# The opening of a cross attention: where the first rows, the constant rows and the first weights stand in the queues

## The chip, the cores and the metric

The program runs on one core of a Trainium2 chip. The metric is device microseconds for one execution. The kernel before took 2498.39 us (median of 3 runs, 2496.61 to 2503.72). The execution that the profiler recorded took 2492.11 us; its span, from the first to the last instruction, is 2490.3 us.

## The reference

Eight sequences of 512 rows and 512 columns pass through a gated cross attention (16 heads of 32 columns, a bias by relative position, a key mask) and then a gated second block with its own attention and a mixture of experts:

```
x = x + tanh(g_xattn) * Wo(softmax(Q K^T / sqrt(32) + bias[q - k], masked) V)
      with Q = layernorm(x) Wq + bq,  K = ctx Wk + bk,  V = ctx Wv + bv
x = x + tanh(g_ffn) * ffn(layernorm(x))
```

Only the first line matters here, and of it only the work that precedes its first scores.

## The kernel before

The program has three passes, one after the other: pass A is the cross attention, pass B the second attention, pass C the experts. The change is in pass A alone.

Pass A works on one sequence at a time as 64 units (16 heads, in 4 groups of 4, by 4 tiles of 128 keys). Each body of the program has 64 steps. In a step TensorE does one unit's scores, one product for a row minimum of a later unit ("max" in the code, L721), and a piece of a job that prepares the next sequence. Jobs are: XT and CT (transposes of the normalised rows and of the context, four tiles each, L629), Q, K and V (products in four pieces of three matmuls, and one matmul for the bias, L654 and L656), and, later, O, M and SP. The table `plan` gives each job its steps and one of three PSUM banks. TensorE takes jobs in the order of their steps, and one that waits holds up all behind it.

The bodies are called "first" (preparation of sequence 0 only, with max products from step 48), "zero" (units of sequence 0), "steady", "last" and "end". "First" is the opening: it loads rows, splits the four weight matrices into a high and a low half (ScalarE w_hi, L420; VectorE w_lo, L508), makes XT, CT, Q, K, V, and hands Q and K group by group to SyncE. `keep` (L240) stores the two halves of a group to DRAM, waits for that, and `stack` (L248, L253) loads them back three times into `q_stack` and `k_stack`, from which scores and max products read. These stacks also hold constant rows that are loaded once from `side_rows` (L313: one partition; L314: 31 partitions, 496 KB; L315: 22 partitions, 352 KB). Each row of such a source is read 16 times, once for each head.

SyncE issues every load and store of pass A but a few in program order: rows, biases, Wq, Wk, mask, rows again as their two buffers come free, Wv and Wo as the weight buffers come free, mask rows, the constant rows, then `keep` and `stack` by group, the band of the bias (2 MB, L328, after group 0), eight one-row loads (L333, after group 1). The body "zero" begins on SyncE with the loads of the next sequence's rows (L233), which VectorE's statistics need at step 4. GpSimd issues four strip loads of 512 KB and casts them.

Of the kernel before, what the change touches and what calls it, by code (L numbers as in the profile page):

```python
# [19 lines left out]
F32 = mybir.dt.float32  # L20
# [8 lines left out]
P = 128  # L29
# [32 lines left out]
def pass_a(nc, x, ctxt, maskb, g_gate, wq, bq, wk, bk, wv, bv, wo, bo, strips, bands, far, side_rows, ident, x1, mask_rows,  # L62
           qk_rows):

    with ExitStack() as ctx:
# [44 lines left out]
        stats = sb("stats", [P, 2, 6])  # L110
        mv = sb("mv", [P, 2, 2])
        rstd = sb("rstd", [P, 2, 3])
# [7 lines left out]
        mask_stage = o_hi[:, 0, :]  # L120
        far_stage, far_hi, far_lo = den[0:NT * H, :], o_lo[0:NT * H, 0, :], o_lo[0:NT * H, 1, :]
# [11 lines left out]
        c_loaded = [sem(f"c_loaded{i}") for i in range(2)]  # L133
        kept = [sem(f"kept{i}") for i in range(2)]
# [30 lines left out]
        pieces = {j: at for j, at, _ in plan}  # L165
        bank_of = {j: job_bank[i] for j, _, i in plan}
        place = {j: i for j, _, i in plan}
# [5 lines left out]
        done_order = {kind: sorted(js, key=lambda j: (pieces[j][-1], names.index(j))) for kind, js in present.items()}  # L173
# [27 lines left out]
        def ended(kind, step):  # L201
            return [j for j in done_order[kind] if pieces[j][-1] == step]
# [22 lines left out]
        MOMENTS = ((4, 7), (6, 9), (15, 18), (17, 20))  # L225
        SPLITS = (10, 16, 23, 25)
# [4 lines left out]
        def _(sp):  # L231
# [30 lines left out]
            def body(kind, b, u):  # L262
                more, own, late_too = kind in ("first", "zero", "steady"), kind in ("zero", "steady", "last"), kind in ("steady", "last", "end")
                if more:
                    for t in range(2):
                        if kind != "first":
                            sp.wait_ge(job_done, before(kind, b))
# [31 lines left out]
                if more:  # L299
# [5 lines left out]
                if more:  # L305
# [38 lines left out]
        def _(pool):  # L344
            def deviation(b, t):
# [4 lines left out]
                nc.gpsimd.tensor_scalar(rstd[:, t % 2, 0:1], mv[:, t % 2, 1:2], EPS, None, ALU.add).then_inc(rstd_step, 1)  # L350
                pool.wait_ge(rstd_step, done + 1)
                nc.gpsimd.tensor_tensor(rstd[:, t % 2, 1:2], rstd[:, t % 2, 0:1], power[:], ALU.pow).then_inc(rstd_step, 1)
                pool.wait_ge(rstd_step, done + 2)
                pool.nop(nofuse=True)
                nc.gpsimd.tensor_scalar(rstd[:, t % 2, 2:3], mv[:, t % 2, 0:1], rstd[:, t % 2, 1:2], -1.0, ALU.mult, ALU.mult
                                        ).then_inc(rstd_step, 1)

            def body(kind, b, u):
                if kind == "zero":
                    pool.wait_ge(far_stored, 16 * 2 * NT)  # L360
                for step in range(STEPS):
# [13 lines left out]
                    if kind in ("first", "zero", "steady"):  # L375
                        for t, (_, at) in enumerate(MOMENTS):
                            if step == at - 2:
                                deviation(b, t)
                    if kind == "first" and step in (MOMENTS[1][1], MOMENTS[2][1], MOMENTS[3][1], 3 * GS):
                        strips_of((MOMENTS[1][1], MOMENTS[2][1], MOMENTS[3][1], 3 * GS).index(step))  # L380
# [28 lines left out]
            for g in range(2):  # L409
                load_strips(g)  # L410
            pool.wait_ge(const_loaded, 16 * (1 + B))
            nc.gpsimd.tensor_scalar(mask_stage, mask8, MASKED, None, ALU.mult).then_inc(mask_set, 1)
# [4 lines left out]
        def _(act):  # L417
# [5 lines left out]
            def evict(kind, b, u, job):  # L423
# [5 lines left out]
                src = bank_of[job][:]  # L429
# [18 lines left out]
            def body(kind, b, u):  # L448
# [4 lines left out]
                for step in range(STEPS):  # L453
# [11 lines left out]
                    for g in range(NG):  # L465
                        if (M, g) in present[kind] and step == pieces[M, g][0] + 1:
# [3 lines left out]
                    if kind in ("first", "zero", "steady"):  # L470
                        for t, (_, at) in enumerate(MOMENTS):
                            if step == at:
                                act.wait_ge(rstd_step, (b + 1) * (NT * 3) + t * 3 + 3)
                                nc.scalar.activation(xn[:, t % 2, :], xn[:, t % 2, :], ACT.Identity, scale=rstd[:, t % 2, 1:2],
                                                     bias=rstd[:, t % 2, 2:3]).then_inc(xn_ready, 1)
# [22 lines left out]
            act.wait_ge(b_loaded, 128)  # L498
# [6 lines left out]
        def _(dve):  # L505
# [6 lines left out]
            def evict(kind, b, job):  # L512
# [4 lines left out]
                src = bank_of[job][:]  # L517
# [30 lines left out]
            def moments(b, t):  # L548
                dve.wait_ge(x_loaded[t % 2], (b + 1) * 32 + 16 * (t // 2 + 1))
                nc.vector.bn_stats(stats[:, t % 2, :], xn[:, t % 2, :]).then_inc(stats_done, 1)  # L550
                dve.wait_ge(stats_done, (b + 1) * NT + t + 1)
                dve.nop(nofuse=True)
                nc.vector.bn_aggr(mv[:, t % 2, :], stats[:, t % 2, :]).then_inc(mv_done, 1)

            def body(kind, b, u):
                if kind == "zero":
                    dve.wait_ge(band_loaded, 16)
                for step in range(STEPS):
# [23 lines left out]
                    if kind in ("first", "zero", "steady"):  # L582
                        for t, (at, _) in enumerate(MOMENTS):
                            if step == at:
                                moments(b, t)
                    if kind == "first" and step in SPLITS:
                        split(SPLITS.index(step))
                        if step == SPLITS[-1]:
# [4 lines left out]
                    for job in ended(kind, step - 1):  # L593
# [5 lines left out]
            dve.wait_ge(b_split, 2)  # L599
            nc.vector.scalar_tensor_tensor(out=b_lo, in0=bstage[DH:DH + 1], scalar=WS, in1=b_lo, op0=ALU.mult,  # L600
                                           op1=ALU.subtract).then_inc(b_split, 1)
# [3 lines left out]
        def _(pe):  # L605
            mm = nc.tensor.matmul

            def free(kind, b, job):

                mine = [j for j in names if j in present[kind] and place[j] == place[job]]  # L610
                prior = [j for j in mine if pieces[j][0] < pieces[job][0]]
                if prior:
                    last = max(prior, key=lambda j: pieces[j][-1])
                    assert pieces[last][-1] < pieces[job][0], (last, job)
# [6 lines left out]
            def transposes(kind, b, job):  # L621
                m, t = job
                src = cn if m == CT else xn
                if m == CT:
                    pe.wait_ge(c_loaded[t % 2], (b + 1) * 32 + 16 * (t // 2 + 1))
                else:
                    pe.wait_ge(xn_ready, (b + 1) * NT + t + 1)
                for k in range(NK):
                    last = nc.tensor.transpose(bank_of[job][:, k * P:(k + 1) * P], src[:, t % 2, k * P:(k + 1) * P], idn[:])  # L629
                last.then_inc(job_done, 1)  # L630

            def product(kind, b, job, k):

                m, n = job
                o, c = bank_of[job][:], slice(n * P, (n + 1) * P)
# [22 lines left out]
            def spread(kind, b, job):  # L658
# [3 lines left out]
                for hh in range(HG):  # L662
                    last = mm(bank_of[job][hh * DH:(hh + 1) * DH, :], ones_f[:], acc[:, hh, :], start=True, stop=True,
# [3 lines left out]
            def turn_low(kind, b, job):  # L667
# [3 lines left out]
                for i in range(NT):  # L671
                    last = nc.tensor.transpose(bank_of[job][0:HG, i * P:(i + 1) * P], low[:, g % 2, i * HG:(i + 1) * HG], idn[:])
                last.then_inc(job_done, 1)

            def fill(kind, b, step):

                for job in names:
                    if job not in present[kind]:
                        continue
                    for k, at in enumerate(pieces[job]):  # L680
# [1774 lines left out]
```

## Time and profile before

| | |
|---|---|
| median of 3 runs | 2498.39 us |
| profiled execution | 2492.11 us, span 2490.3 us |
| TensorE busy | 2193.2 us, 88% of the span |
| TensorE busy in the first 120 us | 59.92 us |
| TensorE busy from 120 to 200 us | 73.89 of 80 us |
| first max product | at 76.31 us |
| first max product of body "zero" | at 93.61 us |

A row of the timeline gives start, duration, engine, line, operation, output and inputs, and in brackets the idle time before it with what ended it. SPq is SyncE issuing a DMA; the duration is that of the issue, not that of the transfer. A row of the windows gives busy time and count for each engine, then the granted clock (1.00 is 2.4 GHz, 0.50 is 1.2 GHz), the mean busy share of the 16 DMA engines (one engine alone is 0.06), and the rate.

### The profile page before, as it was taken

What the parts mean: (1) busy time and instruction counts of PE and PEld (TensorE: products, weight loads), DVE (VectorE), ACT (ScalarE), POOL (GpSimd) and SP (SyncE); (2) the same over time, 40 slices, a digit from 0 to 9 for tenths busy, and PEclk for the clock granted to TensorE, in tenths of its full rate; (3) what the DMA queues carried; (4) which work ended last, traced back from release to release, by engine and by line L of the source; (5) the groups of instructions that cost most, each with busy time, mean ns of one, the idle gap of its engine ahead of it and who ended that gap; (6) DMA issues with size and microseconds to landing.
All of it is one profiled execution on the core that took longest, in us unless ns stands there. A gap on an engine that the chain in (4) does not pass through costs nothing. (4 is left out here: it accounts for less than half of the span.)

```text
span 2490.3 us, 50414 instructions
## 1 busy us (share of the span) xinstructions
PE 2193.2 (88%) x12864; PEld 977.9 (39%) x12865; DVE 1506.9 (61%) x4072; ACT 1201.2 (48%) x2316; POOL 1401.2 (56%) x1598
## 2 busy tenths in 40 slices
PE   3699999999999963899999999999948887898887
PEld 1233333333333211444444444444424443444443
DVE  4588888887888733656655566565526783333332
ACT  3255555555555433354544545455445653444443
POOL 3177767677676751365654655546534664555554
PEclk9899999999999986999999999999978898999999
DMA  4413223232232204452533524334234764555554
GB/s 155 151 48 111 90 87 109 72 107 96 86 116 71 71 26 130 140 147 86 151 118 111 147 90 146 116 118 130 80 107 86 165 148 91 97 93 93 94 92 79
DMA packets 221402, 264.60 MB, mean 106 GB/s; under 512 B 37400, under 2 KB 163468, under 8 KB 220852
## 3 DMA queue, kind: packets, MB, share of 16 engines
q1 hardware_dynamic: 197628, 212.81, 28.2%
q0 software_dynamic: 22976, 48.38, 11.3%
q8 instruction: 106, 1.74, 0.3%
q14 instruction: 172, 1.41, 0.2%
q10 hardware_dynamic: 520, 0.27, 0.0%
HBM read 162.12 MB, written 86.80 MB: 100 GB/s over the span
## 5 line engine op out<-in xcount | busy, mean ns | idle before, releaser
L464 ACT ACTIVATE a_pt<-a_bank 128x512 f32<-128x512 f32 x512 | 305.1, 597 | 361.2 <-DVE a_bank L567 349.2
L1345 DVE CUSTOM_DVE_ANT_0 b_bank<-b_bank,b_tri 128x256 f32<-128x256 f32 (+3 forms) x512 | 253.7, 498 | 322.2 <-PE b_bank L1483 319.8
L578 DVE CUSTOM_DVE_ANT_0 a_bank<-a_bank,a_strip 128x512 f32<-128x512 f32 x512 | 354.8, 693 | 21.5 <-PE a_bank L721 18.8
L1130 POOL TENSOR_TENSOR b_acc<-b_acc,b_pt 128x256 f32<-128x256 f32 (+2 forms) x384 | 271.7, 725 | 105.6 <-ACT b_pt L1219 88.9
L374 POOL TENSOR_TENSOR a_acc<-a_acc,a_pt 128x512 f32<-128x512 f32 x256 | 317.6, 1271 | 12.8 <-ACT a_pt L464 9.3
L567 DVE TENSOR_TENSOR a_bank<-a_bank,a_band 128x256 f32<-128x256 f32 (+1 forms) x512 | 205.9, 403 | 132.3 <-PE a_bank L708 130.5
L1219 ACT ACTIVATE b_pt<-b_bank 128x256 f32<-128x256 f32 (+2 forms) x384 | 143.3, 381 | 203.5 <-PE b_bank L1467 199.5
L721 PE MATMUL a_bank<-a_k_stack,a_q_stack 97*128 97x512 f16 x512 | 197.7, 387 | 17.5 <-DMA a_k_stack<-mask_rows 10.7
L708 PE MATMUL a_bank<-a_q_stack,a_k_stack 128*128 128x512 f16 x512 | 197.6, 387 | 15.4 <-ACT a_pt L464 11.4
L1812 POOL DMA_INDIRECT out_dram<-c_z,c_to_row x72 | 115.1, 1598 | 144.1 <-DMA out_dram<-c_z,c_to_row 117.0
L2203 DVE SCALAR_TENSOR_TENSOR c_hid<-c_th,c_bank 128x256 f32<-128x256 f32 x72 | 30.3, 421 | 229.6 <-ACT c_th L1954 228.2
L1465 PE MATMUL b_bank<-b_q_stack,b_k_stack 96*128 96x256 f16 (+3 forms) x512 | 155.5, 304 | 8.7 <-ACT b_pt L1219 7.8
L371 POOL TENSOR_TENSOR a_acc<-a_pt 128x512 f32<-128x512 f32 x128 | 160.0, 1271 | 5.3 <-ACT a_pt L464 4.9
L1482 PE MATMUL b_bank<-b_k_stack,b_q_stack 96*128 96x256 f16 (+3 forms) x512 | 154.5, 302 | 5.0 <-DMA b_q_stack<-qk_rows 2.7
L388 POOL TENSOR_TENSOR a_o_un<-a_o_un,a_den 128x512 f32<-128x512 f32 x32 | 40.8, 1275 | 204.1 <-DVE a_den L534 204.1
L1145 POOL TENSOR_TENSOR b_o_un<-b_o_un,b_den 128x512 f32<-128x512 f32 x32 | 40.7, 1273 | 201.6 <-DVE b_den L1313 195.6
L1467 PE MATMUL b_bank<-b_q_stack,b_k_stack 97*128 97x256 f16 (+3 forms) x512 | 153.3, 300 | 0.0
L1483 PE MATMUL b_bank<-b_k_stack,b_q_stack 96*128 96x256 f16 (+3 forms) x512 | 153.0, 299 | 0.0
L1927 ACT ACTIVATE c_z<-c_z,c_entry 128x512 f32<-128x512 f32 x72 | 51.9, 721 | 192.9 <-DMA c_z<-z_all,c_from_row 192.9
L735 PE MATMUL a_bank<-a_pt,a_v 128*32 128x512 f32 x1024 | 138.5, 613 | 1.1 <-ACT a_pt L464 1.1
L708 PEld LDWEIGHTS a_bank<-a_q_stack,a_k_stack 128*128 128x128 f16 x512 | 49.5, 97 | 186.3 <-ACT a_pt L464 117.5
L1219 ACT ACTIVATE b_acc<-b_bank 128x512 f32<-128x512 f32 x128 | 76.4, 597 | 94.4 <-PE b_bank L1467 94.3
(337 smaller groups left out, 5632.7 us busy)
## 6 DMA issues: line engine op xcount, KB each, us to landing
b_q_stack<-qk_rows SPq DMA_DIRECT2D x192, 128.0 KB, 2.7
a_q_stack<-qk_rows SPq DMA_DIRECT2D x96, 128.0 KB
a_k_stack<-qk_rows SPq DMA_DIRECT2D x96, 128.0 KB
b_k_stack<-qk_rows SPq DMA_DIRECT2D x96, 128.0 KB, 2.6
a_xn<-in_x SPq DMA_DIRECT2D x32, 256.0 KB, 2.6
a_cn<-in_ctx SPq DMA_DIRECT2D x32, 256.0 KB, 3.1
qk_rows<-a_qk_hi SPq DMA_DIRECT2D x64, 128.0 KB, 1.7
qk_rows<-a_qk_lo SPq DMA_DIRECT2D x64, 128.0 KB, 1.8
```

What stands on the lines that cost most here:

```text
L371: nc.gpsimd.tensor_tensor(acc[:, hh, :], pt[:, (n - HG) % SLOTS, :], mine, ALU.add).then_inc(pooled, 1)
L374: nc.gpsimd.tensor_tensor(acc[:, hh, :], acc[:, hh, :], mine, ALU.add).then_inc(pooled, 1)
L464: nc.scalar.activation(pt[:, n % SLOTS, :], st_bank[n % 2][:], ACT.Exp).then_inc(exped, 1)
L567: nc.vector.tensor_tensor(st_bank[n % 2][:, c0:c1], st_bank[n % 2][:, c0:c1], band[:, h, at:at + c1 - c0], ALU.add).then_inc(biased, 1)
L578: nc.vector.tensor_tensor_reduce(out=max_bank[step % 2][:], in0=max_bank[step % 2][:], in1=strip[:, g * HG + hh, at:at + S], scale=-1.0, s ...
L708: mm(st_bank[n % 2][:], k_stack[:, h, j * P:(j + 1) * P], q_stack[:, h, :], start=True, stop=True).then_inc(scored, 1)
L721: mm(max_bank[step % 2][:], q_stack[0:MASK + 1, h, i * P:(i + 1) * P], k_stack[0:MASK + 1, h, :], start=True, stop=True).then_inc(maxed, 1)
L1130: nc.gpsimd.tensor_tensor(sums_of, sums_of, probs(n), ALU.add).then_inc(pooled, 1)
L1219: nc.scalar.activation(probs(n), st_bank[n % 2][:, 0:w], ACT.Exp).then_inc(exped, 1)
L1345: nc.vector.tensor_tensor_reduce(out=max_bank[step % 2][:, 0:w], in0=max_bank[step % 2][:, 0:w], in1=tri[:, at:at + w], scale=-1.0, scalar ...
L1465: mm(o, k_stack[0][0:LOW, h, j * P:(j + 1) * P], q_stack[0][0:LOW, h, j * P:], start=True, stop=False)
L1482: mm(o, q_stack[0][0:LOW, h, c], k_stack[0][0:LOW, h, 0:w], start=True, stop=False)
```

## The change

Only the body "first" is different in what it issues; the other bodies keep their plan.

- All eight row tiles of sequence 0 are loaded at once: the third and fourth of x go to `sums`, those of the context to the upper halves of `o_hi` and `o_lo`. Order on SyncE: four x tiles, Wq, four context tiles, Wk, gate, mask, far rows, the constant rows, Wv, and then `keep` of Q group 0.
- The biases are loaded by four DMAs from ScalarE's queue instead of eight from SyncE's.
- Statistics of the four x tiles come at steps 0 to 3, and VectorE does them before the low half of the biases. GpSimd issues its first strip loads after them and does all strips in one go.
- A plan of its own: XT at steps 4 to 7, Q group 0 at 8, CT at 12 to 15, then K, V, Q, K, V, Q, K at steps up to 47, V group 2 at 50 to 56, on six banks.
- `stack` of Q group 0 comes before the mask rows and Wo are issued, and the wait for the mask rows stands before `stack` of K.

```
+        first_plan = [((XT, 0), [4], 0), ((XT, 1), [5], 1), ((XT, 2), [6], 2), ((XT, 3), [7], 3), ((Q, 0), run(8), 4),
...
+        places = job_bank + st_bank + [out_bank]
...
-        SPLITS = (10, 16, 23, 25)
+        FIRST_MOMENTS = ((0, 0, 1), (1, 1, 2), (2, 2, 3), (3, 3, 4))
+        SPLITS, LOW_SPLITS = (3, 16, 22, 34), (4, 18, 24, 36)
...
                 if kind == "first":
-                    for n, w in enumerate((bq, bk, bv, bo)):
-                        for row in (0, DH):
-                            sp.dma_start(bstage[row:row + 1, n, :], w.rearrange("(a n) -> a n", a=1)).then_inc(b_loaded, 16)
+                    for t in range(NT):
+                        sp.dma_start(x_tile(kind, t), x[0, t * P:(t + 1) * P, :]).then_inc(x_first[t - 2] if t >= 2 else x_loaded[t], 16)
                     weights(0)
+                    for t in range(NT):
+                        sp.dma_start(c_tile(kind, t), ctxt[0, t * P:(t + 1) * P, :]).then_inc(c_first[t - 2] if t >= 2 else c_loaded[t], 16)
                     weights(1)
...
                 if kind == "first":
-                    weights(2)
-                    weights(3)
-                    sp.wait_ge(mask_set, 1)
-                    sp.dma_start(mask_rows, mask_stage).then_inc(mask_stored, 16)
                     sp.dma_start(q_stack[MASK:MASK + 1, :, :], side_rows[0:1]...).then_inc(sides_stored, 16)
                     sp.dma_start(k_stack[LOW:, :, :], side_rows[1:]...).then_inc(sides_stored, 16)
                     sp.dma_start(q_stack[SIDE + 2 * NT:, :, :], side_rows[SIDE + 2 * NT - MASK:]...).then_inc(sides_stored, 16)
-                    sp.wait_ge(mask_stored, 16)
+                    weights(2)
...
                         keep(kind, b, b + 1, g, part)
+                        if kind == "first" and g == 0:
+                            for i in range(2):
+                                sp.sem_inc((x_loaded, c_loaded)[part][i], 16)
+                            if part:
+                                sp.wait_ge(mask_stored, 16)
                         stack(b + 1, g, part)
+                        if kind == "first" and g == 0 and part == 0:
+                            sp.wait_ge(mask_set, 1)
+                            sp.dma_start(mask_rows, mask_stage).then_inc(mask_stored, 16)
+                            weights(3)
```

The order on SyncE, from the context tiles on, before the change (a_pt is the buffer in which weights land, qk_rows the DRAM copy of Q and K):

```order
L233 DMA a_xn<-in_x 128x512 [waits a_job_done] x2
L233 DMA a_cn<-in_ctx 128x512 [waits a_job_done] x2
L259 DMA a_pt<-in_L_xattn_Wv 128x4x512 [waits a_w_split]
L259 DMA a_pt<-in_L_xattn_Wo 128x4x512 [waits a_w_split]
L312 DMA mask_rows<-a_o_hi 128x512 [waits a_mask_set]
L313 DMA a_q_stack<-in_side_rows 1x16x512
L314 DMA a_k_stack<-in_side_rows 31x16x512
L315 DMA a_q_stack<-in_side_rows 22x16x512
L240 DMA qk_rows<-a_qk_hi 128x512 [waits a_left_dve,a_mask_stored]
```

And the same place after it, from the load of Wk:

```order
L287 DMA a_pt<-in_L_xattn_Wk 128x4x512
L304 DMA a_gate<-in_g_xattn 128x1
L306 DMA a_o_un<-in_mask_BxS_bf 16x128 x8
L307 DMA a_den<-in_beyond 64x512
L337 DMA a_q_stack<-in_side_rows 1x16x512
L338 DMA a_k_stack<-in_side_rows 31x16x512
L339 DMA a_q_stack<-in_side_rows 22x16x512
L287 DMA a_pt<-in_L_xattn_Wv 128x4x512 [waits a_w_split]
L268 DMA qk_rows<-a_qk_hi 128x512 [waits a_left_dve]
L276 DMA a_q_stack<-qk_rows 32x4x512 [waits a_kept0]
L358 DMA mask_rows<-a_o_hi 128x512 [waits a_mask_set]
L287 DMA a_pt<-in_L_xattn_Wo 128x4x512 [waits a_w_split]
```

Wv stood ahead of the 31 constant rows and stands behind them; Wo and the mask rows moved behind the first stack of Q.

On TensorE, where the max products begin, before the change (the products with a_w_hi first are those of V):

```order
L656 MATMUL a_bank<-a_ones,a_bias 128x512
L721 MATMUL a_bank<-a_k_stack,a_q_stack 128x512
L654 MATMUL a_bank<-a_w_hi,a_ct_hi 128x512
L654 MATMUL a_bank<-a_w_lo,a_ct_hi 128x512
L654 MATMUL a_bank<-a_w_hi,a_ct_lo 128x512
L721 MATMUL a_bank<-a_k_stack,a_q_stack 128x512
```

And after it:

```order
L695 MATMUL a_bank<-a_ones,a_bias 128x512
L760 MATMUL a_bank<-a_k_stack,a_q_stack 128x512 x3
L693 MATMUL a_bank<-a_w_hi,a_ct_hi 128x512
L693 MATMUL a_bank<-a_w_lo,a_ct_hi 128x512
L693 MATMUL a_bank<-a_w_hi,a_ct_lo 128x512
L760 MATMUL a_bank<-a_k_stack,a_q_stack 128x512 x2
```

Before, V group 1, Q group 2, K group 2 and V group 2 ran among the 16 max products; now only V group 2 does, and the other three stand ahead of them.

## Rows read from the trace of the kernel before

**Rows 1.** Windows of three stretches of pass A: engines, clock, DMA share, GB/s.
```profile
0.00:120.00 120.00, 59.92 (x244) 26.93 (x245) 54.89 (x105) 34.12 (x45) 30.10 (x44) 0.91 0.48 152
...
120.00:200.00 80.00, 73.89 (x396) 27.64 (x397) 66.43 (x183) 45.00 (x80) 57.49 (x52) 0.98 0.21 65
200.00:1100.00 900.00, 816.84 (x4393) 317.30 (x4392) 672.94 (x1810) 450.76 (x809) 572.85 (x551) 0.95 0.30 95
```

**Rows 2.** Waits of TensorE in the first 120 us, longest in total first.
```profile
PE a_bank L629 <- ACT a_xn L474: 22.6, 1, 22.6
PE a_bank L629 <- DVE a_xt_lo L545: 14.4, 4, 6.5
PE a_bank L721 <- DMA a_k_stack<-mask_rows: 10.7, 1, 10.7
PE a_bank L721 <- DVE a_low L578: 6.8, 2, 6.0
```

**Rows 3.** Timeline of SyncE's queue, 36 to 76 us.
```profile
37.50 0.44 SPq L314 DMA_DIRECT2D a_k_stack<-in_side_rows  x1
37.99 21.41 SPq L315 DMA_DIRECT2D a_q_stack<-in_side_rows  x1
59.51 1.14 SPq L240 DMA_DIRECT2D qk_rows<-a_qk_hi  x1
...
68.90 1.29 SPq L248 DMA_DIRECT2D a_q_stack<-qk_rows  x3
...
73.06 1.29 SPq L248 DMA_DIRECT2D a_k_stack<-qk_rows  x3
...
74.72 0.35 SPq L328 DMA_DIRECT2D a_band<-in_bands  x1
```

**Rows 4.** Windows of the DMA load, same columns as rows 1.
```profile
0.00:16.00 16.00, 0.00 (x0) 0.01 (x1) 2.90 (x4) 5.10 (x3) 1.63 (x8) 1.00 0.85 278
...
40.00:42.00 2.00, 1.66 (x8) 1.56 (x8) 0.28 (x1) 0.51 (x1) 1.70 (x3) 1.00 0.60 220
...
46.00:48.00 2.00, 0.00 (x0) 0.00 (x0) 2.00 (x1) 1.14 (x3) 0.00 (x0) 1.00 0.06 20
...
66.00:68.00 2.00, 0.00 (x0) 0.00 (x0) 0.00 (x0) 0.26 (x1) 0.00 (x0) 1.00 0.07 24
```

**Rows 5.** Timeline of the split of Wk, on ScalarE and VectorE.
```profile
31.65 1.90 ACT L420 ACTIVATE a_w_hi<-a_pt 128x2048 f16<-128x2048 f32 x1
...
33.59 2.29 DVE L508 SCALAR_TENSOR_TENSOR a_w_lo<-a_pt,a_w_hi 128x2048 f16<-128x2048 f32 x1 [1.11 <-ACT a_w_hi L420]
```

**Rows 6.** Timeline of TensorE and VectorE around the first max products.
```profile
76.31 0.61 PE L721 MATMUL a_bank<-a_k_stack,a_q_stack 97*128 97x512 f16 x1 [10.68 <-DMA a_k_stack<-mask_rows]
...
82.56 0.38 PE L654 MATMUL a_bank<-a_w_hi,a_ct_lo 128*128 128x512 f16 x1
82.77 0.38 PE L656 MATMUL a_bank<-a_bias,a_ones 128*128 128x512 f16 x1
...
93.61 0.60 PE L721 MATMUL a_bank<-a_k_stack,a_q_stack 97*128 97x512 f16 x2
...
84.39 0.70 DVE L578 CUSTOM_DVE_ANT_0 a_bank<-a_bank,a_strip 128x512 f32<-128x512 f32 x1
...
86.12 0.70 DVE L578 CUSTOM_DVE_ANT_0 a_bank<-a_bank,a_strip 128x512 f32<-128x512 f32 x1
```

**Rows 7.** Windows of the two stretches at a lowered clock.
```profile
76.00:82.00 6.00, 5.69 (x14) 2.09 (x15) 2.82 (x7) 0.00 (x0) 0.00 (x0) 0.50 0.86 317
...
106.00:113.00 7.00, 4.20 (x10) 1.30 (x11) 5.78 (x17) 3.35 (x6) 2.11 (x6) 0.52 0.38 132
```

**Rows 8.** Timeline of SyncE, VectorE and TensorE at the next sequence's rows.
```profile
104.00 0.35 SPq L233 DMA_DIRECT2D a_xn<-in_x  x1
...
100.52 0.14 DVE L578 DVE_READ_ACCUMULATOR2_ANT a_low<- 128x1 f32 x1
107.01 0.69 DVE L550 BATCH_NORM_STATS2 a_stats<-a_xn 128x6 f32<-128x512 f32 x1 [6.35 <-DMA a_xn<-in_x]
```

More of the change, by code:

```diff
@@ L133, in pass_a @@
         c_loaded = [sem(f"c_loaded{i}") for i in range(2)]
+        x_first = [sem(f"x_first{i}") for i in range(2)]
+        c_first = [sem(f"c_first{i}") for i in range(2)]
         kept = [sem(f"kept{i}") for i in range(2)]
@@ L164, in pass_a, with pieces, place, bank_of @@
                 ((K, 2), run(56), 0), ((V, 2), [60, 60, 61, 61], 1)]
-        pieces = {j: at for j, at, _ in plan}
-        bank_of = {j: job_bank[i] for j, _, i in plan}
-        place = {j: i for j, _, i in plan}
+        first_plan = [((XT, 0), [4], 0), ((XT, 1), [5], 1), ((XT, 2), [6], 2), ((XT, 3), [7], 3), ((Q, 0), run(8), 4),
+                      ((CT, 0), [12], 5), ((CT, 1), [13], 0), ((CT, 2), [14], 1), ((CT, 3), [15], 2), ((K, 0), run(18), 3),
+                      ((V, 0), run(24), 1), ((Q, 1), run(28), 0), ((K, 1), run(32), 2), ((V, 1), run(36), 1), ((Q, 2), run(40), 0),
+                      ((K, 2), run(44), 2), ((V, 2), [50, 52, 54, 56], 1)]
+        places = job_bank + st_bank + [out_bank]
+        plans = {kind: {j: (at, i) for j, at, i in (first_plan if kind == "first" else plan)}
+                 for kind in ("first", "zero", "steady", "last", "end")}
+        def pieces(kind, j):
+            return plans[kind][j][0]
+        def place(kind, j):
+            return plans[kind][j][1]
+        def bank_of(kind, j):
+            return places[place(kind, j)]
         names = [j for j, _, _ in plan]
@@ L201, in ended @@
         def ended(kind, step):
[L202 removed]
+            return [j for j in done_order[kind] if pieces(kind, j)[-1] == step]
         def adds(n):
@@ L224, in pass_a, with moments_at, x_tile, c_tile @@
         STEPS = UNITS
-        MOMENTS = ((4, 7), (6, 9), (15, 18), (17, 20))
-        SPLITS = (10, 16, 23, 25)
+        MOMENTS = ((4, 5, 7), (6, 7, 9), (15, 16, 18), (17, 18, 20))
+        FIRST_MOMENTS = ((0, 0, 1), (1, 1, 2), (2, 2, 3), (3, 3, 4))
+        SPLITS, LOW_SPLITS = (3, 16, 22, 34), (4, 18, 24, 36)
+        def moments_at(kind):
+            return {"first": FIRST_MOMENTS, "zero": MOMENTS, "steady": MOMENTS, "last": (), "end": ()}[kind]
+        def x_tile(kind, t):
+            return x_spare[t - 2] if kind == "first" and t >= 2 else xn[:, t % 2, :]
+        def c_tile(kind, t):
+            return c_spare[t - 2] if kind == "first" and t >= 2 else cn[:, t % 2, :]
         block = ctx.enter_context(nc.Block())
@@ L298, in body @@
                         stack(b, G3, part)
-                if more:
+                if kind in ("zero", "steady"):
                     for m, t in ((XT, 0), (XT, 1), (CT, 0)):
@@ L304, in body @@
                     store(0)
-                if more:
+                if kind in ("zero", "steady"):
                     sp.wait_ge(job_done, upto(kind, b, (CT, 1)))
@@ L374, in body @@
                             nc.gpsimd.tensor_tensor(acc[:, hh, :], acc[:, hh, :], mine, ALU.add).then_inc(pooled, 1)
[L375 to L380, printed above, removed]
+                    for t, (_, at, _) in enumerate(moments_at(kind)):
+                        if step == at:
+                            deviation(b, t)
+                    if kind == "first" and step == FIRST_MOMENTS[-1][1]:
+                        for g in range(2):
+                            load_strips(g)
+                        pool.wait_ge(const_loaded, 16 * (1 + B))
+                        nc.gpsimd.tensor_scalar(mask_stage, mask8, MASKED, None, ALU.mult).then_inc(mask_set, 1)
+                        for g in range(NG):
+                            strips_of(g)
                     g, off = divmod(step, GS)
@@ L469, in body @@
                                           ).then_inc(m_stacked[g], 16)
[L470 to L475, printed above, removed]
+                    for t, (_, _, at) in enumerate(moments_at(kind)):
+                        if step == at:
+                            act.wait_ge(rstd_step, (b + 1) * (NT * 3) + t * 3 + 3)
+                            nc.scalar.activation(x_tile(kind, t), x_tile(kind, t), ACT.Identity, scale=rstd[:, t, 1:2],
+                                                 bias=rstd[:, t, 2:3]).then_inc(xn_ready, 1)
                     if kind == "first" and step in SPLITS:
@@ L581, in body @@
                                                        accum_out=low[:, g % 2, i * HG + hh:i * HG + hh + 1]).then_inc(lowered, 1)
[L582 to L588, printed above, removed]
+                    for t, (at, _, _) in enumerate(moments_at(kind)):
+                        if step == at:
+                            moments(kind, b, t)
+                    if kind == "first" and step == FIRST_MOMENTS[-1][0]:
+                        dve.wait_ge(b_split, 2)
+                        nc.vector.scalar_tensor_tensor(out=b_lo, in0=bstage[DH:DH + 1], scalar=WS, in1=b_lo, op0=ALU.mult,
+                                                       op1=ALU.subtract).then_inc(b_split, 1)
+                    if kind == "first" and step in LOW_SPLITS:
+                        split(LOW_SPLITS.index(step))
+                        if step == LOW_SPLITS[-1]:
                             dve.wait_ge(gate_ready, 1)
```

77 lines of the change are left out of this document (39 added, 38 removed).

## The prediction

> **What bounds the kernel now.** I read the windows first: the first 120 us keep TensorE busy for 59.92 us, the next 80 for 73.89, and the 900 after that for 816.84 [rows 1]. Past the opening TensorE is the bound, and its work there is not touched, so whatever the opening saves moves everything behind it earlier. Next the waits of TensorE in those 120 us: 22.6 us until the first normalised tile, 14.4 for single evictions between transposes, 10.7 before the first max product, 6.8 near the start of body "zero" [rows 2]. The last two are the ones that stand directly before work that nothing can overtake, so the question is what releases them.
>
> Then SyncE's timeline. It issues the 31 constant rows at 37.50 and then needs 21.41 us to issue the 22 rows. So `keep` of Q group 0 is issued at 59.51, and its `stack` only at 68.90; K follows at 73.06 and the band at 74.72 [rows 3]. The windows of the DMA load tell what it waited for: from 46 to 60 us, in seven windows of 2 us, and again from 64 to 68, the 16 engines are busy to 0.06 to 0.07, one sixteenth, at 20 to 24 GB/s [rows 4]. One engine alone carries the 31 rows. Its backlog begins when the bulk loads end, at about 41 (the window 40 to 42 falls to 0.60), and ends just before 68.3, as the stack starts at 68.90: 27.3 us. SyncE is released at 59.4, 18.4 us after that beginning. I call this one engine's backlog the lane.
>
> The Trainium skill ("DMA: Bandwidth & Descriptors", "Why a DMA increments its semaphore by 16 and not by 1") says that a transfer spreads over the largest number of engines, at most 16, that divides its slowest dimension, and over the lowest-numbered ones. By that rule 31 partitions give one engine and 22 give eleven; the trace agrees with its 0.07 of 16.
>
> **The change part by part.**
>
> *Rows, statistics, biases, own plan.* TensorE's 22.6 us wait for the first tile and the 14.4 us between transposes shrink or go. I cost this at nothing, gained or lost, for the lane covers it. Even if Wk were split no earlier than before, at 33.59 + 2.29 = 35.9 [rows 5], and Q and K group 0 ran only then, 26 matmuls at the slow pace of 0.446 us that rows 6 show (below), they would be done at 47.5, when Wv lands. Without that cover this part would be worth up to the 16 us by which Q and K can be ready before 47.
>
> *Constant rows ahead of Wv and of `keep`.* They wait for nothing now, so the lane begins when the bulk ahead of it has passed. The first 16 us moved 278 GB/s x 16 us = 4.4 MB before [rows 4]; now x, ctx, Wq and Wk are 4 MB, with 0.3 MB of small loads and part of 1 MB of strips. I take 16 us again, as the start of the lane. It lasts 27.3 us, plus one more strip load's sixteenth, 32 KB at 24 GB/s = 1.3 us (two fall into it now, one did before). Wv's sixteenth is 64 KB, 2.7 us, and `keep`, 16 KB or 0.7 us of the 27.3, is now behind it. That a transfer behind the lane waits for it is in the rows: `keep`, issued at 59.51, has landed only at 68.90, while the other engines have nothing from 64 on [rows 3, 4]. Wv has landed at 16 + 27.3 + 1.3 + 2.7 - 0.7 = 46.6, say 47 us. SyncE itself is stuck until 16 + 18.4 + 1.3 = 36; it could not issue Wv before, and Wv's other fifteen parts are in by about 42. The gain is that the lane ends near 45 instead of 68; the price is that Wv, which landed before the lane, now lands after it.
>
> *From Wv to the first max product.* After it ScalarE w_hi 1.90 and VectorE w_lo 2.29 follow one another [rows 5]: 47 + 4.3 with the hand-overs = 51.3. Then V, Q, K, V, Q, K stand in TensorE's order before step 48: 6 x 13 = 78 matmuls. From 82.56 to 93.61 there are 51 starts, 0.217 us each [rows 6]: 16.9 us. TensorE has idled before, as it had before 76.31, where the granted clock was 0.50, its 1.2 GHz level [rows 7], and 14 starts took 6.25 us instead of 3.0 [rows 6]: 3.2 more. The first max product comes at 51.3 + 16.9 + 3.2 = 71.4, before at 76.31: **4.9 us gained**. `stack` of K does not hold it: Q is kept at about 47.7, stacked at 49, mask rows and Wo are issued at 50, `keep` of K at 51; 1.8 MB at the 278 GB/s of the first stretch is 6.5 us, so `stack` of K is issued at 57.5 and lands near 60. The same queue held the wait for mask rows before; those are stored by then.
>
> *The 16 max steps.* Before, 52 matmuls of four jobs ran among them, from 76.31 to 93.61: 17.3 us. Now 13. VectorE sets the pace: two steps from 84.39 to 86.12, 0.865 us each [rows 6], 16 of them 13.8 us. **3.5 us gained**, and body "zero" begins at 85.2 instead of 93.61.
>
> *The next sequence's rows.* Before, SyncE reached them at 104.00, and VectorE stood 6.35 us from 100.66 to 107.01 [rows 8]. From the band at 74.72 to 107.01 is 32.3 us, and nearly all of it is SyncE's own chain (band, two groups, eight one-row loads), which the change leaves as it is. It starts at about 58 now, and the rows are in at 90.3. VectorE needs them 7.0 us after the first max product of "zero", at 92.2. **6.35 us gained**, with 1.9 us to spare; if the chain is later than that, it takes back what it is late.
>
> *The clock after that stall.* The stretch 106 to 113 had 10 matmuls at 0.52 [rows 7], 2.0 us slower than at full rate; VectorE was busy for 5.78 of the 7 us, so I count half, **1.0 us gained**.
>
> *Rest.* ScalarE's four bias DMAs, the later strips (needed at 71) and the split of Wo (issued at 50, due at about 60) lie beside the lane or the six jobs. Semaphore increments, other banks: nothing measurable, bounded by 0 and the 0.7 us of one hand-over each side. None of them stands last before TensorE.
>
> Sum: 4.9 + 3.5 + 6.35 + 1.0 = 15.7 us. Against the profiled execution 2492.11 - 15.7 = 2476.4; the median of before lies 6.3 us above that execution, so I give 2498.39 - 15.7 = **2482.7 us**.
>
> Unknown costs, both ends. The lane: 496 KB at 24 GB/s would be 20.7 us instead of 27.3, which gives 6.6 us more; with all four strips in it and half the surplus again it is 34 us, which takes 6.7 us away, from the first max product and (less the 1.9) from the stall. I keep 27.3, the measured length. Start of the lane: 14 to 18 us. The slow clock before V group 0: 0 to 3.2 us, I take 3.2.
>
> The same page ("Queues, rings and completion order") says that each engine takes its ring's entries in order. By it Wv's sixteenth sits behind the 31 rows, and the trace agrees, as `keep` does [rows 3, 4]; without it Wv would be in at 42, and the sum 18 us, since the next sequence's rows would then be late by 2.8. It speaks against a change that puts Wv there.
>
> **The rivals.**
>
> One: the lane is short, or Wv does not share it. For it: 496 KB at the rate seen make 20.7 us only. Then Wv lands at 42, the max products begin at 66.4, and SyncE's chain ends at 86 to 90. The gain is 18 to 22 us: about 2478. Against it: the measured 27.3.
>
> Two: the lane is longer, because four strip loads and the end of the bulk loads fall into it. Every us goes through at full price at the first max product, and after 1.9 us also at the next rows, but there it replaces, not adds. With a lane end 8 us later the gain is 15.7 - 8 = 8: 2490.7. For it: the first 16 us moved at 0.85 of the engines, so something always shares engine 0.
>
> Three: no change. The early Q and K are of no use, SyncE holds Wv until far later than 36, and Wv lands at 60. TensorE would begin the max products at 84, but the stall and the 3.5 us are still won: 15.7 - 13 = 2.7 us gained, 2495.7.
>
> Four, on the other side: Wv behind the lane makes it slower. It is the place of Wv in the queue: 47 us now, while it stood ahead of the lane before. The point from which this decides is Wv landing at 47 + 15.7 = 63; it is slower by 0.3% from 70. For that the lane must run at half the measured rate, 12 GB/s, 55 us: Wv at 74, gain 15.7 - 27 = -11: 2510. For it: the transfer's 27.3 us against 20.7 by bytes show that sharing costs. Against it: seven windows at a constant 24 GB/s.
>
> **How the numbers follow.** My forecast (gain 12 to 18 us) has 0.50, rival one 0.19, rival two 0.18, rival three 0.08, rival four 0.05. A measurement of this kernel can tell about 0.3%, 7.5 us. Faster by more than that: 0.50 + 0.19 + 0.16 of two = 0.85; within it: the rest of two, three and a part of four, 0.12; slower 0.03. The range: rival one's end and the lane's lower bound give 2473; two gives 2491, and some of three is taken in up to 2493.
>
> **What would show it.** Right: the issue of the 22 rows again lasts about 20 us, from 12.7 on; a stretch of 0.07 DMA share between 20 and 45; TensorE idle until about 51, then six jobs in a row, the first of them at a clock of 0.5; first max product at 71, "zero" at 85; no wait of the statistics for rows in "zero". Wrong: a first max product released by a DMA of `k_stack` instead of by K group 2 (then SyncE's chain decides, not Wv); a stall of the statistics of more than 3 us; Wv in before 42 or after 55; or a stretch after 200 us that takes longer than before.

## The result, and the profile after

The changed kernel takes 2486.34 us (median of 6 runs, 2480.95 to 2491.43), the kernel before, run beside it, 2498.19 us (6 runs, 2493.34 to 2503.72). The ratio is 0.995 with an interval of 0.9932 to 0.9969: it is faster by 11.9 us, less than the 15.7 forecast and inside the range. The profiled execution took 2480.95 us with a span of 2479.2, 11.1 us less than before.

The windows answer to [rows 1].

```profile
0.00:120.00 120.00, 70.40 (x296) 29.63 (x297) 62.49 (x137) 40.55 (x58) 40.67 (x57) 0.87 0.51 161
120.00:200.00 80.00, 77.60 (x418) 28.20 (x417) 66.63 (x184) 45.30 (x81) 56.41 (x51) 1.00 0.24 77
200.00:1100.00 900.00, 816.75 (x4431) 319.44 (x4430) 669.76 (x1805) 454.18 (x818) 571.35 (x546) 0.96 0.31 96
```

TensorE's busy time from 200 to 1100 us is the same as before, 816.75 against 816.84. The whole difference lies in the first 200 us, where more work is done earlier. SyncE's timeline, and then windows of the DMA load, against [rows 3, 4]:

```profile
14.04 0.50 SPq L338 DMA_DIRECT2D a_k_stack<-in_side_rows  x1
14.58 24.13 SPq L339 DMA_DIRECT2D a_q_stack<-in_side_rows  x1
38.75 1.30 SPq L287 DMA_DIRECT2D a_pt<-in_L_xattn_Wv  x1
...
52.38 1.29 SPq L276 DMA_DIRECT2D a_q_stack<-qk_rows  x3
...
92.17 0.35 SPq L261 DMA_DIRECT2D a_xn<-in_x  x1
```

```profile
18.00:20.00 2.00, 1.05 (x3) 0.44 (x4) 0.89 (x2) 0.00 (x0) 0.56 (x1) 1.00 0.70 230
20.00:22.00 2.00, 2.00 (x6) 0.69 (x5) 0.00 (x0) 0.00 (x0) 2.00 (x3) 1.00 0.11 41
22.00:24.00 2.00, 2.00 (x10) 0.97 (x9) 0.00 (x0) 0.06 (x1) 2.00 (x2) 1.00 0.07 24
...
34.00:36.00 2.00, 2.00 (x6) 0.76 (x5) 0.00 (x0) 0.00 (x0) 1.32 (x2) 0.50 0.07 24
...
48.00:50.00 2.00, 0.00 (x0) 0.00 (x0) 0.00 (x0) 0.00 (x0) 0.00 (x0) 0.50 0.07 26
```

The backlog of the one engine now begins right behind the bulk loads, at about 19.5 (the window 18 to 20 still has 0.70), and still holds at 48 to 50, with Wv's sixteenth at its end. Wv was issued at 38.75 and is not in before 51.6. The Trainium skill's rule that each engine takes its ring's entries in order ("DMA: Bandwidth & Descriptors", "Queues, rings and completion order") agrees with this.

The timeline of ScalarE, VectorE and TensorE from the eviction of K group 0 to the first exponential:

```profile
36.81 0.60 ACT L471 ACTIVATE a_qk_hi<-a_bank 128x512 f16<-128x512 f32 x1 [8.53 <-PE a_bank L695]
51.66 1.91 ACT L453 ACTIVATE a_w_hi<-a_pt 128x2048 f16<-128x2048 f32 x1 [14.25 <-DMA a_pt<-in_L_xattn_Wv]
...
53.60 2.29 DVE L542 SCALAR_TENSOR_TENSOR a_w_lo<-a_pt,a_w_hi 128x2048 f16<-128x2048 f32 x1 [15.47 <-ACT a_w_hi L453]
...
55.99 0.58 PE L693 MATMUL a_bank<-a_w_hi,a_ct_hi 128*128 128x512 f16 x1 [19.22 <-issue]
...
75.05 0.60 PE L760 MATMUL a_bank<-a_k_stack,a_q_stack 97*128 97x512 f16 x2
...
87.03 0.38 PE L760 MATMUL a_bank<-a_k_stack,a_q_stack 97*128 97x512 f16 x1 [0.39 <-DVE a_low L615]
...
95.35 0.69 DVE L587 BATCH_NORM_STATS2 a_stats<-a_xn 128x6 f32<-128x512 f32 x1 [1.02 <-DMA a_xn<-in_x]
...
97.34 0.60 ACT L497 ACTIVATE a_pt<-a_bank 128x512 f32<-128x512 f32 x1 [8.04 <-DVE a_bank L604]
```

ScalarE waited 14.25 us for Wv and nothing else. TensorE had Q and K of group 0 done and then stood for 19.22 us. The view puts this down to "issue", but its first matmul starts 0.1 us after w_lo ends (53.60 + 2.29). The first max product follows 78 matmuls later with no wait for a stack, where before it waited 10.7 us for one [rows 2].

One correction to what stands ahead. The row at 93.61 [rows 6] holds the last two max products of "first", not the first of "zero". There are 16 of them from 76.31, two of them in that row, and the first one of "zero" is this, in the timeline of the kernel before:

```profile
95.04 0.38 PE L721 MATMUL a_bank<-a_k_stack,a_q_stack 97*128 97x512 f16 x1 [0.83 <-DVE a_low L578]
...
109.00 0.60 ACT L464 ACTIVATE a_pt<-a_bank 128x512 f32<-128x512 f32 x1 [12.01 <-DVE a_bank L567]
```

So the 16 steps took 18.7 us before, not 17.3. With it the gain adds up as follows (all times in us, read off the two profiled executions):

| stretch | before | after | gained | forecast |
|---|---|---|---|---|
| start to first max product | 76.31 | 75.05 | 1.3 | 4.9 |
| 16 max steps | 18.7 | 12.0 | 6.7 | 3.5 |
| "zero" to the statistics of the next rows | 12.0 | 8.3 | 3.7 | 6.35 |
| to the first exponential | 2.0 | 2.0 | 0.0 | |
| from there to the end of the span | | | -0.6 | 1.0 |
| sum | | | 11.1 | 15.7 |

### The profile page after: what moved, and what is told of

Its sections match the earlier page's. It is cut to its first block and busy times, and to the rows that moved or that the text cites. A ratio compares the mean times of both kernels' runs of the same rounds, so it can differ in the third digit from the quotient of the medians.

```text
span 2479.2 us, 50415 instructions
## 1 busy us (share of the span) xinstructions
PE 2192.0 (88%) x12864; PEld 976.4 (39%) x12865; DVE 1503.3 (61%) x4072; ACT 1200.4 (48%) x2316; POOL 1401.9 (57%) x1598
## 5 line engine op out<-in xcount | busy, mean ns | idle before, releaser
L407 POOL TENSOR_TENSOR a_acc<-a_acc,a_pt 128x512 f32<-128x512 f32 x256 | 317.8, 1271 | 10.7 <-ACT a_pt L497 7.5
```

The lines of the kernel that those rows point to most:

```text
L407: nc.gpsimd.tensor_tensor(acc[:, hh, :], acc[:, hh, :], mine, ALU.add).then_inc(pooled, 1)
```

## The experiments

The theory: the backlog of one DMA engine (the lane) decides when Wv is in, and with it everything up to the first max product. Its rivals: the gain comes from the early x and Q whatever the lane does; SyncE's own chain (`keep`, `stack`, band, next rows) decides; or the lane's length, not its place, is all that counts. Ratios are against the kernel before on the same chip: for the first four kernels its median is 2496.78 us (22 runs), for the others 2497.07 (11 runs). Beside the changed kernel it was 2498.19, so a plain difference from the changed kernel's median comes out 1.1 to 1.4 us larger than one taken through the kernel before.

### The lane spread over all engines

```
-  sp.dma_start(k_stack[LOW:, :, :], side_rows[1:]...broadcast_to([P - LOW, H, S]))
+  sp.dma_start(k_stack[LOW:LOW + 16, :, :], side_rows[1:17]...broadcast_to([16, H, S]))
+  sp.dma_start(k_stack[LOW + 16:, :, :], side_rows[17:]...broadcast_to([P - LOW - 16, H, S]))
```

The 31 rows become 16 and 15, with TensorE waiting for one more increment. In the changed kernel:

> The changed kernel with the 31 constant rows loaded by two DMAs, 16 rows and 15 rows, instead of one. Theory (one engine's backlog decides): the stretch with a DMA share of 0.07 disappears, SyncE issues the 22 rows in under 1 us, Wv has landed by 26 instead of 51.66, the first max product comes at about 60 instead of 75.05, the statistics of the next sequence at about 79 instead of 95.35, and the time falls by 14 to 18 us against the changed kernel. Rival (what held Wv was the bulk of bytes before it, not one engine): Wv lands 5 us earlier at most and the time falls by under 5 us.

Measured: 2471.42 us (6 runs, 2468.29 to 2476.53), ratio 0.99 (0.9883 to 0.9918), so 14.9 us below the changed kernel (13.5 if each is taken against the kernel before that ran beside it). The 22-row issue takes 0.31 us, and Wv is no longer what ScalarE waits for (SyncE's queue, then ScalarE and VectorE):

```profile
14.42 0.31 SPq L340 DMA_DIRECT2D a_q_stack<-in_side_rows  x1
16.80 0.40 SPq L287 DMA_DIRECT2D a_pt<-in_L_xattn_Wv  x1
...
36.97 0.60 ACT L472 ACTIVATE a_qk_hi<-a_bank 128x512 f16<-128x512 f32 x1 [8.32 <-PE a_bank L696]
37.46 1.90 ACT L454 ACTIVATE a_w_hi<-a_pt 128x2048 f16<-128x2048 f32 x1
...
81.02 0.69 DVE L588 BATCH_NORM_STATS2 a_stats<-a_xn 128x6 f32<-128x512 f32 x1 [0.32 <-DMA a_xn<-in_x]
...
83.01 0.60 ACT L498 ACTIVATE a_pt<-a_bank 128x512 f32<-128x512 f32 x1 [7.65 <-DVE a_bank L605]
```

w_hi comes 14.2 us earlier than after the change (37.46 against 51.66), now right behind the eviction of K group 0, and the first exponential 14.3 us earlier. This shows the lane as the bound of the changed opening. The trace agrees with the Trainium skill's rule on the number of engines ("DMA: Bandwidth & Descriptors", "Why a DMA increments its semaphore by 16 and not by 1"), which the prediction cited: sixteen partitions go over sixteen engines, and of the long stretch of 0.07 one window of 0.08 is left, at 34 to 36.

The same edit in the kernel before:

> The kernel before with the same split of the 31 rows. Theory: Q group 0 is kept at 57 instead of 68.9, the first max product comes at about 66 instead of 76.31, SyncE's chain then ends with the next sequence's rows at about 95 instead of 107.01, and the time falls by about 12 us (9 to 14), as much as the whole change gave. Rival (the gain of the change came from its early x and Q): the split alone gives under 4 us.

Measured: 2487.13 us (10 runs, 2482.85 to 2495.42), ratio 0.9964 (0.9949 to 0.9978), 9.7 us gained. The first max product is at 66.47, released by the mask rows of the stack after 1.16 us, and the statistics of the next rows still wait (VectorE):

```profile
96.71 0.70 DVE L551 BATCH_NORM_STATS2 a_stats<-a_xn 128x6 f32<-128x512 f32 x1 [8.88 <-DMA a_xn<-in_x]
```

The four kernels make a square: without the split the change is worth 11.9 us, with it 2487.13 - 2471.42 = 15.7. The split is worth 9.7 before and 13.5 after, each against its own kernel before. The profiled executions say the same by the time of the first exponential (109.00 before, 98.70 with the split, 97.34 changed, 83.01 changed with the split): the change is worth 11.7 and 15.7, the split 10.3 and 14.3. The 3.8 us between 11.9 and 15.7 are less than the intervals of these medians can tell, so that the lane covers part of the change's worth rests on one execution of each kernel.

The rival's own mark, under 4 us for the split alone, is missed. But the square does not take the early x and Q out of the account: with the lane spread in both kernels, the other parts of the change still gain 15.7. No run has the early rows with the constant rows left at their old place, so how the 11.9 us divide between the rows, the plan and the place of the lane is not shown.

### Place of the lane: Wv ahead of it

```
 if kind == "first":
+    weights(2)
     sp.dma_start(q_stack[MASK:MASK + 1, :, :], ...)
     ...
-    weights(2)
```

> The changed kernel with Wv issued ahead of the constant rows, nothing else. Theory that SyncE's chain stands just behind Wv: V group 0 follows K group 0 at once and the first max product comes at about 65.5 instead of 75.05, but stack of K group 0 stays at 62 and the next sequence's rows still arrive at 95 to 97, so the time stays within 2 us of the changed kernel's. Rival (Wv alone decides, as the prediction's sum has it): the time falls by about 9 us.

Measured: 2487.32 us (7 runs, 2481.89 to 2491.58), ratio 0.996 (0.9945 to 0.9976), which overlaps the changed kernel's 0.9932 to 0.9969: no change that can be told. The first max product comes at 68.47, 6.6 us earlier than in the changed kernel, but the stall comes back:

```profile
93.24 0.69 DVE L587 BATCH_NORM_STATS2 a_stats<-a_xn 128x6 f32<-128x512 f32 x1 [5.68 <-DMA a_xn<-in_x]
```

5.68 us of waiting instead of 1.02: what Wv gives, SyncE's chain takes. With Wv out of the lane the statistics begin only 2.1 us earlier (93.24 against 95.35), and the first exponential, too, at 95.22 instead of 97.34. So the lane holds the changed kernel at two places, and freeing one of them brings out the other.

### The lane early in the kernel before

```
     sp.dma_start(far_stage, far).then_inc(far_loaded, 16)
+    (the three loads of constant rows)
     ...
     sp.dma_start(mask_rows, mask_stage).then_inc(mask_stored, 16)
-    (the three loads of constant rows)
```

> The kernel before with only one part of the change: the three DMAs of constant rows stand behind the far rows and ahead of the second half of the rows, Wv and Wo. Theory: the one-engine backlog runs from 16 to 44, but SyncE is stuck in it until about 38, so the third row tile arrives about 17 us later than before, Q group 0 is evicted near 70, and the time rises by about 3 us (0 to 7): the early place pays only with all rows loaded ahead. Rival (the early place is by itself the gain): the time falls by 10 us or more.

Measured: 2502.38 us (10 runs, 2498.16 to 2505.47), ratio 1.0019 (1.0007 to 1.0032), 5.6 us slower. SyncE's queue says why:

```profile
13.29 20.37 SPq L282 DMA_DIRECT2D a_q_stack<-in_side_rows  x1
33.70 2.43 SPq L233 DMA_DIRECT2D a_xn<-in_x  x1
```

The third x tile is behind the stuck issue, VectorE waits 16.38 us for it, and the first exponential comes at 112.42 instead of 109.00. Moving the constant rows forward alone is a loss; in the change all eight row loads stand ahead of them.

### Both behind the lane moved: Wv first and the next rows early

```
-  if kind in ("zero", "steady"):
+  if kind == "steady":
       (loads of the next rows)
   ...
   if kind == "first" and g == 1:
+      sp.wait_ge(job_done, upto("first", -1, (CT, NT - 1)))
+      for t in range(2):
+          load(x, xn, x_loaded, 0, t)
+          load(ctxt, cn, c_loaded, 0, t)
```

This stands on top of the kernel with Wv first.

> The changed kernel with Wv ahead of the constant rows, and with the first four row loads of the next sequence issued after the stacks of group 1 and before the one-row loads, instead of at the end of SyncE's chain. Theory (with Wv first, SyncE's chain is the next limit): the 5.68 us stall of the statistics goes, the first exponential comes at about 89.5 instead of 95.22, and the time falls by 4 to 6 us against the kernel with Wv first alone. Rival (those rows were late for another reason, such as the queue's bytes): under 1.5 us.

Measured: 2479.72 us (5 runs, 2476.19 to 2479.98), ratio 0.9925 (0.991 to 0.994): 7.6 below the kernel with Wv first, more than the 4 to 6 expected. The statistics have no wait at all, at 91.75. But in this execution the issue of the 22 rows lasted 25.25 us, and Wo came late on ScalarE's timeline:

```profile
61.92 1.91 ACT L457 ACTIVATE a_w_hi<-a_pt 128x2048 f16<-128x2048 f32 x1 [12.65 <-DMA a_pt<-in_L_xattn_Wo]
...
64.35 0.57 ACT L475 ACTIVATE a_qk_hi<-a_bank 128x512 f16<-128x512 f32 x1
```

The evictions of Q, V and K stand behind this split in ScalarE's order, and TensorE waited 10.4 us for them. So the first max product is at 72.61 and the first exponential at 93.73 instead of the 89.5 expected. That the rows were the second bound is shown by the wait that is gone. In this execution Wo's split is the third. The size is not explained: the first exponential is only 1.5 us earlier than with Wv first (95.22), and the two profiled executions differ by 2.2 us (2481.89, the lowest of its seven, and 2479.72), where the medians differ by 7.6. The lane differs from execution to execution (below).

### The strips' share of the lane

```
-  for g in range(2):
-      load_strips(g)
   pool.wait_ge(const_loaded, 16 * (1 + B))
   nc.gpsimd.tensor_scalar(mask_stage, mask8, MASKED, None, ALU.mult)...
+  pool.wait_ge(mask_stored, 16)
+  for g in range(2):
+      load_strips(g)
```

In the changed kernel GpSimd issued 1 MB of strips at 13.59, just ahead of the lane. Here they wait until the mask rows are stored.

> The changed kernel with the four strip loads of 512 KB issued only after the mask rows are stored, so that none runs before or beside the 31 constant rows. Theory (the term that was too small in the prediction is the strips' share on the one engine, 128 KB at 24.5 GB/s): Wv lands 5 us earlier, at about 46.5, the first max product comes at about 70 instead of 75.05; the strips then collide with Wo, so the chain gains less, and the first exponential comes 2 to 4 us earlier. Rival (the backlog is as long without them): Wv lands within 1 us of 51.66.

Measured: 2480.38 us (6 runs, 2477.32 to 2485.84), ratio 0.9931 (0.9915 to 0.9946), 6.0 below the changed kernel. That interval overlaps the changed kernel's 0.9932 to 0.9969, so a gain in time is not shown. What the run can show is in its timeline, with Wv's split and the statistics:

```profile
46.44 1.91 ACT L454 ACTIVATE a_w_hi<-a_pt 128x2048 f16<-128x2048 f32 x1 [7.37 <-DMA a_pt<-in_L_xattn_Wv]
...
93.51 0.69 DVE L588 BATCH_NORM_STATS2 a_stats<-a_xn 128x6 f32<-128x512 f32 x1 [5.12 <-DMA a_xn<-in_x]
```

Wv is in 5.2 us earlier, and the first max product is at 69.31, 5.7 us earlier. The first exponential moves by 1.85 us only, because the statistics wait 5.12 us again. The profiled execution, 2485.84 us, is the slowest of the six and no faster than the changed kernel's median.

### The way to a faster kernel

On top of the spread lane: the next rows early, as above, and V group 1, Q group 2 and K group 2 put back between the max products.

```
-  ((V, 1), run(36), 1), ((Q, 2), run(40), 0), ((K, 2), run(44), 2), ((V, 2), [50, 52, 54, 56], 1)]
+  ((V, 1), run(48), 1), ((Q, 2), run(52), 0), ((K, 2), run(56), 2), ((V, 2), [60, 60, 61, 61], 1)]
```

> The changed kernel with the 31 rows split in two DMAs, the early row loads, and V group 1, Q group 2 and K group 2 back among the 16 max products as before the change. Theory (six jobs ahead of the max products cost more than they save, since VectorE's 0.75 to 0.87 us a step leaves room for three matmuls): the max products begin at about 53 instead of 61.42, the first of body zero at 69 instead of 73.4, the first exponential at about 78.5 instead of 83.01, and the time falls by 3 to 6 us against the split alone. Rival (the jobs slow the max steps by as much as they come earlier): within 1.5 us.

Measured: 2464.71 us (4 runs, 2460.89 to 2467.06), ratio 0.9864 (0.9846 to 0.9882), 6.7 below the spread lane alone (whose interval begins at 0.9883) and 21.6 below the changed kernel. The early rows and the other order of the jobs were not tried one without the other here. The first max product is at 52.51, as expected, but the 16 steps took 19.8 us, since VectorE had other work ahead of them:

```profile
52.33 2.29 DVE L547 SCALAR_TENSOR_TENSOR a_w_lo<-a_pt,a_w_hi 128x2048 f16<-128x2048 f32 x1 [1.11 <-ACT a_w_hi L458]
54.54 0.15 DVE L635 TENSOR_SCALAR a_gate<-a_gate 128x1 f32<-128x1 f32 x1
54.60 0.67 DVE L637 TENSOR_TENSOR a_o_lo<-a_den,a_o_lo 64x512 f16<-64x512 f32 x1
```

TensorE waited 2.2 us for VectorE, and the granted clock of 56 to 60 was 0.58. So the first exponential, 79.73, is 3.3 us earlier than with the spread lane, where 4.5 were expected.

Last, Wv ahead of the constant rows in this kernel:

> All of these together: the split, Wv ahead of the constant rows, early row loads, jobs among the max products. Theory: V group 0 follows K group 0 at 37 without a wait, the max products begin when K group 0 is stacked, at about 50, the first exponential comes at about 75, and the time is 6 to 9 us under the split alone, near 2463. Rival (K group 0's stack and the 31 rows share the same bytes, so Wv first only moves the wait): no more than split, rows and jobs give without Wv first.

Measured: 2465.57 us (4 runs, 2462.85 to 2469.88), ratio 0.9869 (0.9852 to 0.9886): no difference, as the rival forecast. The theory's times did not come: the first max product is at 53.59 instead of 50 and the first exponential at 80.75 instead of 75, both 1.0 to 1.1 us later than without the move. The rival's reason, shared bytes, was not tested. In the rows ScalarE splits Wv right behind the eviction of K group 0 in both kernels, so an earlier Wv has no taker. Once the lane is spread, Wv's place in the queue costs nothing that can be told.

## Why the prediction was right, and where it was not

**The bound: right.** The first max product was released by the jobs behind Wv, and Wv by the lane. Spreading the lane alone took 13.5 to 14.9 us away, and no other single edit of the changed kernel took as much. The issue of 22 rows lasted about 20 us as forecast (24.13), the 0.07 windows are there, TensorE idled and began at the slow clock. The price named in the prediction, that Wv now lands after the lane and not before it, is real: with Wv ahead of the lane the first max product comes at 68.47, 6.6 us earlier.

**The lane's start: the term that was mis-sized.** The prediction took 16 us for the start, the value of the kernel before. The windows show the bulk ending at about 19.5, 3.5 us later. In the kernel before, the first two strip loads were issued at 1.35 and lay within the first 16 us. Now they are issued at 13.59, just ahead of the lane, and 4.3 + 1 MB at the prediction's 278 GB/s make an estimated 19 us. The third and fourth (24.65 and 28.98) fall into the lane, as the prediction had it: one is in its 27.3 us, one it added as 1.3. The sum with the true start gives 46.6 + 3.5 = 50.1, and Wv's split began at 51.66; the last 1.5 us are less than the lane differs from one execution to the next. All four strips together are 128 KB on the lane's engine, an estimated 5.2 us at the 24 to 26 GB/s of the windows. Held back, they gave that back: 46.44. The first term was 1.3 instead of 4.9. That is rival two at half its size.

**From Wv to the first max product: right.** Forecast 16.9 + 3.2 = 20.1 us for 78 matmuls, measured 75.05 - 55.99 = 19.1. The 3.2 us for the slow clock came from a miscount: from 76.31 to 82.56 there are 15 starts in the timeline before, not 14, so the slow pace is 0.417 us and not 0.446. Here the slow start cost 19.1 - 16.9 = 2.2 us.

**The 16 max steps: right in kind, wrong in size, twice.** They began at a mis-read end (18.7 us before, not 17.3), 1.4 us to the good. And the pace of 0.865 us was not VectorE's, as the prediction put it. It is TensorE's: one max product and three matmuls of a job at 0.217 us each make 0.87, and in 14 of the 16 steps before there stood job matmuls. VectorE alone does a step in 0.65 to 0.70, as these three of the changed kernel show, and in the changed kernel 12 of the 16 steps have no job; the mean is 12.0 / 16 = 0.75.

```profile
84.08 0.70 DVE L615 CUSTOM_DVE_ANT_0 a_bank<-a_bank,a_strip 128x512 f32<-128x512 f32 x1
...
84.77 0.70 DVE L615 CUSTOM_DVE_ANT_0 a_bank<-a_bank,a_strip 128x512 f32<-128x512 f32 x1
...
85.43 0.70 DVE L615 CUSTOM_DVE_ANT_0 a_bank<-a_bank,a_strip 128x512 f32<-128x512 f32 x1
```

The four slow steps at 1.2 GHz before [rows 7] are gone too, as the forecast had it, since the clock rises in V group 0 now. The gain was 6.7 instead of 3.5.

**The stall of the next rows: gone but for 1.02 us.** Forecast were rows at 90.3 and need at 92.2. SyncE issued them at 92.17 and the statistics began at 95.35. SyncE's chain is late by the lane, not by Wv: the band was issued at 63.74 where 58 was forecast, and with Wv first the chain stayed nearly where it was and the wait is 5.68. The need is later than forecast as well. The 7.0 us behind the first max product of "zero" were counted from the mis-read 93.61; from 95.04 they are 5.6. In the changed kernel they are 7.3, from 87.03 to 94.33. What the stretch gained, 3.7 us, is less than the 5.3 that the stall lost, and the rest is a stretch at a lowered clock which the prediction did not have, the windows of 88 to 92 in the changed kernel:

```profile
88.00:92.00 4.00, 4.00 (x14) 1.59 (x13) 1.32 (x5) 0.59 (x1) 0.00 (x0) 0.60 0.54 167
```

Before, this part of "zero" (95 to 107) ran at a granted clock of 0.97. Ahead of the fall TensorE had gone through the steps without jobs, waiting for VectorE at nearly every one. This is the row of its waits in the first 120 us; one of the 12, 0.64 us at 97.11, lies behind the fall, so that 11 waits with 3.5 us in total stand ahead of it:

```profile
PE a_bank L760 <- DVE a_low L615: 4.2, 12, 0.7
```

The other kernels sort the same way. In the 4 us that begin about 1 us after the first max product of "zero", the granted clock was 0.57 with the spread lane, 0.66 with Wv first, 0.57 with the next rows early as well and 0.70 with the strips held back, all with the same steps without jobs. It was 1.00 in that place in the kernel before, in its two variants, and in the last two kernels, all of which have jobs among the steps. That the waiting itself brings the clock down was not tried alone. The term of 1.0 us for the clock after the stall did not show: behind the first exponential nothing more was gained, and 0.6 us were lost up to the end of the span.

**Order of the rivals.** Rival one (short lane) and rival four (slower) are excluded by the windows and the time. Rival three is excluded by Wv, which is in at 51.6 and not at 60; how much the early Q and K are worth by themselves stays open, as said at the square. The forecast was 3.8 us too high in gain: 3.6 and 2.7 and 1.6 too much in the three terms above (first max, stall, clock and rest), and 3.2 too little in the max steps, which leaves 4.6 for the profiled span. That the total came so close is in part luck: of 7.9 us too much, 3.2 were made up by a misread row and a pace taken too slow.

## What to carry to other kernels

A load over 31 partitions made one engine a queue of its own here. Look for windows of 0.06 to 0.07 and for an issue of 20 us on the next DMA, and cut the load into 16 and the rest before moving anything around it. An early place in a queue is worth only what stands behind it. Row loads behind the lane cost 5.6 us, and Wv behind it held the first max product back by 6.6 us; putting Wv back gained no time until the next rows were moved as well. When a stretch gets shorter, count who waits in it: in all five kernels here where TensorE waited a little at nearly every step, it ran at a lower clock right after.

## What the runs showed of the hardware that was not expected

The spread lane moves its bytes on all engines, but slowly. The windows of the changed kernel with the split:

```profile
22.00:24.00 2.00, 2.00 (x7) 0.76 (x6) 0.00 (x0) 0.00 (x0) 2.00 (x2) 1.00 1.06 116
24.00:26.00 2.00, 2.00 (x18) 1.70 (x16) 1.07 (x2) 1.70 (x4) 1.70 (x4) 1.00 1.18 103
26.00:28.00 2.00, 0.01 (x1) 0.00 (x0) 2.00 (x4) 2.00 (x3) 2.00 (x2) 1.00 1.03 99
```

The mean share is at 1 (it can come out above 1 in this view), at 99 to 116 GB/s. In the next window, 28 to 30, with what was queued behind, Wv among it, it is 299 at a share of 1.04. One engine alone moved 24 to 26. So the rate in these windows, which hold a strip load as well, is about four times that of one engine, not sixteen times. Whether it is the few destination partitions, or the source row of 1 KB that is read 16 times over, was not tried.

The lane is not of one length. The kernel with Wv first and the one with the next rows early as well are alike in all that SyncE issues up to the constant rows, and the issue that waits for the lane took 22.46 us in the one and 25.25 in the other. So a time of this opening that hangs on the lane is known to some 3 us from one execution, about as much as the smaller steps above. Two executions are all that this rests on.
